# Encoder stage of a fused model: another order of TensorE's products, of the masked state on VectorE and of the query copy on ScalarE

## The reference, cut to what matters

```python
def _phi(t): return jax.nn.elu(t) + 1.0
def layer(h, p):
    q = _phi((h @ wq + bq_).reshape(b, s, H, DH))
    k = _phi((h @ wk + bk_).reshape(b, s, H, DH))
    v = (h @ wv + bv_).reshape(b, s, H, DH)
    kv = jnp.einsum('bshd,bshm->bhdm', k, v)
    z = 1.0 / (jnp.einsum('bshd,bhd->bsh', q, k.sum(axis=1)) + 1e-06)
    att = jnp.einsum('bshd,bhdm,bsh->bshm', q, kv, z).reshape(b, s, d)
    h = h + att @ wo + bo_
    h = _ln(h, g1_, be1_)
    y = jax.nn.gelu(h @ w1 + c1_, approximate=False) @ w2 + c2_
    return (_ln(h + y, g2_, be2_), None)
h, _ = jax.lax.scan(layer, x, params)
return _ln(h, gf, bef)
```

## Time and profile before

| what | value |
|---|---|
| median of 3 runs | 3285.73 us |
| profiled execution: span from its first to its last instruction | 3171.8 us |
| profiled execution's own time | not recorded; the median stands 113.9 us above the span |
| mean granted TensorE clock | 0.897 of full speed |
| first and last projection of the encoder (L3088) | 1516.7 and 2559.8 us |
| TensorE, VectorE, ScalarE, GpSimd busy over the span | 82%, 66%, 57%, 36% |

### The profile page before, as it was taken

One profiled execution on the slowest core, in us unless ns is written; L12 is line 12 of the kernel. 1 busy time (PEld: TensorE's weight loads), 2 busy tenths in 40 slices (PEclk: granted clock), 3 DMA queues, 4 the chain that ended last, 5 costly groups with the idle time before them and its releaser, 6 DMA issues.

```text
span 3171.8 us, 67664 instructions
## 1 busy us (share of the span) xinstructions
PE 2585.6 (82%) x25429; PEld 2010.4 (63%) x25429; DVE 2092.7 (66%) x7713; ACT 1796.5 (57%) x3508; POOL 1149.2 (36%) x1583
## 2 busy tenths in 40 slices
PE   7899988677797693587689999999999867875776
PEld 4466664455576472355578888888888755553555
DVE  6667758843578535533687777777777776336767
ACT  5344446333463342345479988899989744453443
POOL 4200004631754407755642222222222236555412
PEclk9799999789898895689799999999999987896997
DMA  9400000034100252144100000000000001441000
GB/s 276 125 3 3 3 2 1 31 94 135 34 17 25 76 142 65 49 126 138 32 16 13 1 13 13 1 13 13 1 13 1 1 2 42 126 137 28 22 2 28
DMA packets 134053, 147.94 MB, mean 47 GB/s; under 512 B 14817, under 2 KB 109922, under 8 KB 133730
## 3 DMA queue, kind: packets, MB, share of 16 engines
q1 hardware_dynamic: 106306, 71.13, 7.7%
q0 software_dynamic: 27424, 72.48, 7.6%
HBM read 77.63 MB, written 65.93 MB: 45 GB/s over the span
## 4 chain that ended last, share of the span: by engine, by line
PE 59%; DVE 19%; POOL 11%; issue 6%; ACT 4%; DMA 1%; SPq 0%; POOLq 0%; DVEq 0%; ACTq 0%
PE banks L3160 7%; PE banks L3147 5%; POOL results L1351 4%; POOL bins L1152 3%; PE banks L3092 3%; PE banks L3109 2%; PE banks L1900 2%; PE banks L3118 2%; PE banks L546 2%; PE banks L3128 1%; PE banks L3101 1%; PE banks L2926 1%; PE banks L3088 1%; DVE shared_floats L2050 1%; PE banks L2927 1%
## 5 line engine op out<-in xcount | busy, mean ns | idle before, releaser
L3238 POOL TENSOR_SCALAR shared_floats<-shared_floats 128x2 f32<-128x2 f32 x256 | 57.7, 225 | 710.0 <-DVE shared_floats L3229 709.3
L3160 PE MATMUL banks<-layer,shared_floats 128*128 128x128 f32 x2048 | 273.2, 277 | 0.0
L3474 ACT ACTIVATE shared_floats<-banks,layer 128x256 f32<-128x256 f32 x512 | 210.3, 471 | 90.9 <-PE banks L3147 90.9
L3160 PEld LDWEIGHTS banks<-layer,shared_floats 128*128 128x128 f32 x2048 | 251.7, 194 | 0.0
L3147 PE MATMUL banks<-shared_floats,layer 128*128 128x256 f32 x1024 | 243.9, 381 | 0.0
L3250 DVE TENSOR_SCALAR shared_floats<-banks,shared_floats 128x128 f32<-128x128 f32 x512 | 186.3, 405 | 58.7 <-POOL shared_floats L3240 58.7
L1351 POOL DMA_INDIRECT results<-results,result_rows x128 | 124.5, 973 | 256.8 <-DMA results<-shared_floats 219.5
L3226 DVE BATCH_NORM_STATS2 shared_floats<-banks 128x6 f32<-128x128 f32 x512 | 125.9, 287 | 122.3 <-PE banks L3160 118.8
L3147 PEld LDWEIGHTS banks<-shared_floats,layer 128*128 128x128 f32 x1024 | 185.9, 192 | 20.2
L3240 POOL TENSOR_TENSOR shared_floats<-shared_floats,neg_half 128x2 f32<-128x2 f32 x256 | 183.9, 718 | 21.3
L238 PE MATMUL banks<-ident,xn 128*128 128x128 f32 x320 | 65.4, 340 | 138.5 <-issue 74.8
(11 more groups left out here) (393 smaller groups left out, 7993.9 us busy)
## 6 DMA issues: line engine op xcount, KB each, us to landing
bins<-zero SPq DMA_DIRECT2D x1, 18176.0 KB, 86.6
shared_floats<-bins SPq DMA_DIRECT2D x32, 320.0 KB, 4.2
results<-shared_floats SPq DMA_DIRECT2D x32, 320.0 KB, 3.5
expert_weights<-in_dram_experts SPq DMA_DIRECT2D x32, 312.0 KB, 3.1
layer<-in_dram_layers SPq DMA_DIRECT2D x8, 902.0 KB, 4.7
bins<-zero SPq DMA_DIRECT2D x1, 5760.0 KB, 23.6
bins<-xn,f_bin_row POOLq DMA_INDIRECT x256, 2.2
results<-results,result_rows POOLq DMA_INDIRECT x128
```

The costliest lines, as they stand in the source:

```text
L3160: m = T.matmul(to, hidden[:, n * S + t * P:n * S + (t + 1) * P], w["w2"][:, tile(n)], start=False, stop=(n == NF - 1), skip_group_check=True)
L3474: m = A.activation(hidden[:, n * S:(n + 1) * S], k.bank[5 + half][:, part], ACT.Gelu, bias=w["c1"][:, n:n + 1])
```

## The change

On TensorE `project` is split in two: `project_q` now comes before `turn_xn2` and `project_kv` behind it; and the second narrow is split: its transpose and first two products come before `turn_att`, its last two behind it. On VectorE `mask_state(g)` moves from the start of round g+1 to round g, between the two `norm_apply` calls. On ScalarE the first half of `exps_q` becomes `lift_q` and moves ahead of `copy_h`. The work itself is the same.

```diff
--- before.py
+++ after.py
@@ -3075,7 +3075,7 @@
 
     T = k.nc.tensor
 
-    def project(u):
+    def project_q(u):
         w, h = layer_weights(k, u), turned(k, u)
         if u % B == 0:
             T.wait_ge(k.sem(f"e2_layer_in{u // B % 2}"), 16 * (u // B // 2 + 1))
@@ -3086,6 +3086,9 @@
         if u:
             T.wait_ge(k.sem("e2_exp_q"), u)
         T.matmul(k.bank[0][:, LOW], w["wq"], h, start=True, stop=True).then_inc(k.sem("e2_q_made"), 1)
+
+    def project_kv(u):
+        w, h = layer_weights(k, u), turned(k, u)
         if u:
             T.wait_ge(k.sem("e2_kv"), u)
         for t in range(QT):
@@ -3147,7 +3150,8 @@
                 m = T.matmul(k.bank[5 + half][:, part], w["w1"][:, tile(n)], h1[:, :], start=True, stop=True)
             m.then_inc(k.sem("e2_wide"), 1)
 
-    def narrow(u, t):
+    def narrow(u, t, begin=0, end=NF):
+
         w, hidden, h1_c2 = layer_weights(k, u), k.sb("e2_hidden", [P, NF * S]), k.sb(f"e2_h1_c2_{u % 2}", [P, S])
         to = k.bank[7][:, tile(t)]
         if t == 0:
@@ -3155,11 +3159,12 @@
             T.wait_ge(k.sem("e2_gelu"), 2 * u + 2)
             if u:
                 T.wait_ge(k.sem("e2_xn2"), u)
-        T.transpose(to, h1_c2[:, tile(t)], k.ident[:, :])
-        for n in range(NF):
+        if begin == 0:
+            T.transpose(to, h1_c2[:, tile(t)], k.ident[:, :])
+        for n in range(begin, end):
             m = T.matmul(to, hidden[:, n * S + t * P:n * S + (t + 1) * P], w["w2"][:, tile(n)],
                          start=False, stop=(n == NF - 1), skip_group_check=True)
-        if t == QT - 1:
+        if t == QT - 1 and end == NF:
             m.then_inc(k.sem("e2_narrow"), 1)
 
     def turn_xn2(u):
@@ -3188,18 +3193,22 @@
     for g in range(LEAVE + 2 * NC):
         if 1 <= g <= U2:
             sum_states(g - 1)
+        if g < U2:
+            if g > LEAVE:
+                T.wait_ge(k.sem("e2_left"), (g - LEAVE + 1) // 2)
+            project_q(g)
         if 4 <= g < U2 + 4:
             turn_xn2(g - 4)
         if g < U2:
-            if g > LEAVE:
-                T.wait_ge(k.sem("e2_left"), (g - LEAVE + 1) // 2)
-            project(g)
+            project_kv(g)
         if 1 <= g <= U2:
             attend(g - 1)
         if 3 <= g < U2 + 3:
             narrow(g - 3, 0)
         if 2 <= g < U2 + 2:
             turn_xn1(g - 2)
+        if 3 <= g < U2 + 3:
+            narrow(g - 3, 1, 0, NF // 2)
         if 1 <= g <= U2:
             turn_att(g - 1)
         if g < 2 * NC and g % 2 and g // 2 + 1 < NC:
@@ -3208,7 +3217,7 @@
         if g >= LEAVE and (g - LEAVE) % 2 == 0:
             leave((g - LEAVE) // 2)
         if 3 <= g < U2 + 3:
-            narrow(g - 3, 1)
+            narrow(g - 3, 1, NF // 2, NF)
         if 1 <= g <= U2:
             project_out(g - 1)
         if 2 <= g < U2 + 2:
@@ -3378,8 +3387,6 @@
             enter(g // 2 + 1)
         if s.after_routed and g < 2 * NC - 3 and g % 2:
             combine_first(k, s, g // 2 + 2)
-        if 1 <= g <= U2:
-            mask_state(g - 1)
         if g < U2:
             add_bias(g)
         if 1 <= g <= U2:
@@ -3403,6 +3410,8 @@
             norm_apply(k, "e2_xn2", g - 3, k.bank[7])
         if g < 2 * NC - 2 and g % 2 == 0:
             ln_apply(k, s, g // 2 + 1)
+        if g < U2:
+            mask_state(g)
         if 1 <= g <= U2:
             norm_apply(k, "e2_xn1", g - 1, k.bank[3][:, HIGH])
         if 3 * B <= g < 3 * B + 2 * NC and g % 2:
@@ -3428,14 +3437,17 @@
         A.wait_ge(k.sem("ln_turned"), n + 1)
         A.copy(k.sb("e2_hT", [P, N])[:, c * CH:(c + 1) * CH], k.bank[0][:, :]).then_inc(k.sem("ln_xnT"), 1)
 
-    def exps_q(u):
-        w, exp_q, q1 = layer_weights(k, u), k.sb("e2_exp_q", [P, S]), k.sb("e2_q_plus", [P, S])
+    def lift_q(u):
+        w, q1 = layer_weights(k, u), k.sb("e2_q_plus", [P, S])
         if u % B == 0:
             A.wait_ge(k.sem("e2_prepared"), u // B + 1)
         A.wait_ge(k.sem("e2_q_made"), u + 1)
         if u:
             A.wait_ge(k.sem("e2_qk"), u)
         a.count(A.activation(q1[:, :], k.bank[0][:, LOW], ACT.Identity, bias=w["bq1"]))
+
+    def exps_q(u):
+        w, exp_q = layer_weights(k, u), k.sb("e2_exp_q", [P, S])
         A.activation(exp_q[:, :], k.bank[0][:, LOW], ACT.Exp, bias=w["bq"]).then_inc(k.sem("e2_exp_q"), 1)
 
     def exps_k(u):
@@ -3482,6 +3494,8 @@
 
     enter(0)
     for g in range(LEAVE + 2 * NC):
+        if g < U2:
+            lift_q(g)
         if 4 <= g < U2 + 4:
             copy_h(g - 4)
         if g < U2:
```

## The result

The changed kernel takes **3240.72 us** (median of 4 runs, 3223.71 to 3246.47), the kernel before beside it 3284.05 us (4 runs, 3281.26 to 3286.63). That is 43 us faster by the medians. The ratio of the two on record is 0.9836 with an interval of 0.9811 to 0.9861, which makes it 46 to 62 us; the medians alone give 0.9868, just outside. So the change is faster beyond doubt, and its size is known to some 10 us. Forecast were 3242, 3222 to 3265, and faster at 0.91.

The account below looks back on a forecast made before the run. TensorE was taken to bound steady rounds, VectorE the first and last. Gains of 18 + 4.4 + 0.8 + 20.6 = 43.8, taken as 44, cut the span from 3171.8 to 3128; plus 113.9 gave 3242 us, range 3222 to 3265.

Parts of the forecast that it names:

- bias rounds: Eight rounds where VectorE adds L2_final's bias before the mask take 0.55 more; the move hides it, 4.4 us.
- the three old waits: TensorE's waits at turn_xn2 (0.13), turn_att (0.24) and attend (0.05), together 0.42 us a round, would all go.
- The new wait: TensorE before project_out, waiting for ScalarE's attT copy: 0.16 late plus 0.06 restart, taken as 0.25; bounds 0 and 0.43.
- What removes which wait: On TensorE, mask move removes attend's 0.05, query product ahead of turn_xn2 its 0.13, split narrow turn_att's 0.24.
- The edges: First and last rounds, bound by VectorE, gain 0.86 or 1.11 each, mean 0.98; 20.6 us, bounds 8 and 27.
- its three items: VectorE's edge loop: mask slot (0.32) and idle for attend (0.32) leave; xn1 is applied 0.33 or 0.08 later.
- C: Rival, chance 0.04: ScalarE's loop, laid out at 7.50, becomes the bound and the kernel slower, 3372 or 3290.
- Rival A: Wait before project_out as long as the three it replaces; only first and last rounds gain, 26 us: 3260; chance 0.18.
- D: Rival, chance 0.06: neutral, entering rounds give back the steady gain because the mask's wait holds VectorE; some 3286.
- B: Rival, chance 0.10: no wait arises before project_out, ScalarE's copy coming 0.2 earlier; steady rounds 7.3, time 3216.
- The table load: ScalarE, between q and attT copy: the row shows 1.28 us; the skill's 2.66 would make rounds some 8.9.
- What lies outside the span: The median's 113.9 us above the 3171.8 span, placed outside first and last instruction and carried over unchanged.

Follow-up runs that it names:

- second execution: The changed kernel run once more, unaltered, in the second series against the kernel before: 3117.26 us, ratio 0.9818.
- c1_one_ahead: The changed kernel with only the transpose and one product of the second narrow ahead of turn_att, three behind it: 3112.67 us, ratio 0.9800.
- e2_narrow_only: The kernel before with only the second narrow split around turn_att: 3155.33 us, ratio 0.9931.
- e1_mask_only: The kernel before with only mask_state moved: 3160.51 us, ratio 0.9948.
- c2_lift_behind_copy: The changed kernel with ScalarE's lift_q again behind copy_h: 3137.14 us, ratio 0.9881.
- the half widen: The changed kernel with half of widen, four passes of 256 columns, put ahead of project_out in every round: 3101.07 us, ratio 0.9776.

## Why the prediction was right

By its own steps, forecast against measured:

| term | forecast, us | measured, us |
|---|---|---|
| a steady round | 7.54 | 7.53 |
| 105 steady rounds | 18 | 19.8, the rest of the middle |
| bias rounds | 4.4 | 4.4 |
| prepare (one is added to a new layer's biases) | 0.8 | 0.9 (six rounds of 7.86) |
| entering rounds | 11.8 | 11.0 (14.2 in the second execution) |
| leaving rounds and the two before | 8.8 | 8.9 |
| sum | 43.8 | 45.1 |

The mechanism came as forecast: the three old waits gone, one new wait ahead of project_out that ScalarE's attT copy ends, and shorter bias, entering and leaving rounds. That 3242 meets the median of 3240.72 within 2 us is in part luck. The four times of the changed kernel spread over 23 us, the ratio on record makes the gain 54, and the same pair in the second series gained 55.

- *The new wait*: forecast 0.25, measured 0.22 (0.33 less 0.11). The forecast's 0.16 late and 0.06 to restart are these 0.22; the other 0.03 was for ScalarE's slots. The forecast had ScalarE ready at 4.63 and turn_att's result at 4.64. c1_one_ahead shows ScalarE ready 0.10 earlier: ScalarE was not late, turn_att and the copy behind it were the wait. The slots' "up to 0.06 later" did not come.
- *What removes which wait*: this step was wrong, without harm to the sum. I gave the 0.13 to the query product and the 0.05 to the mask. e2_narrow_only shows both gone by the split narrow, by its rows through the new wait itself. Waits that share a loop are not prices to be added: alone, q gives 0.05, the mask 0, the narrow 0.19, and the three together 0.19. The sum held because all three waits go: then the round is TensorE's own 7.29 and the new wait, whichever part removed which. My expectation for q alone was too high by the same mistake.
- *The bias*: right, and shown by e1_mask_only, where bias rounds cost 7.72 and not 8.27.
- *The edges*: right in sum, off in the parts. A leaving round fell from a mean of 10.12 (10.02 and 10.21) to 9.05, 1.07 against a forecast of 0.98; the measure holds seven of them (7.5) and the two before, which gave 1.4 where 1.0 was forecast. The mask alone gave 0.62 (9.5) where its three items come to 0.44, or to 0.56 without the new wait, which that run doesn't have. The narrow alone gave 0.21 (9.91) where I had 0.55; together they give 0.24 more than apart. Entering rounds fell, so the reading of VectorE's loop stands. The mask alone gave 5.7 there and the narrow alone 0.2 (147.0), so there too the parts gave more together than apart.
- *The rivals*: C's loop over ScalarE is real. Laid out at 7.50, it measures 7.42, 0.13 above TensorE's 7.29 and 0.11 below the changed kernel's round. c2_lift_behind_copy makes it the bound at 7.64. Rival A (7.7) and D (entering rounds that lose) are refuted by the rows; B (7.29) is what the half widen brings.
- *The table load*: the earlier trace rows had 1.28 us a load and the exponential 0.02 behind it. It is the same after, with 126 loads of each kind at a mean of 1283 ns. By the 2.66 a switch of the Trainium skill (ScalarE: Activation LUTs, What ACT_TABLE_LOAD costs) ScalarE's loop would be some 10.2 long by estimate (two times 1.38 more); it measures 7.42 in c1_one_ahead, and the measurement decides.
- *What lies outside the span*: this step was wrong. I put the 113.9 us between the span and the median outside the first and last instruction. Every run after shows 1.3 or 1.4 there (3237.99 less 3236.6). The profiled execution of before, at 3171.8, belongs with the times of the experiments (3173 to 3178), not with its own median. Its own time isn't on record, so this is inferred: its encoder starts at 1516.7, as in the experiments (1509.9 to 1533.1), while that of the changed kernel beside the result starts at 1630.1. Carrying the difference over unchanged did no harm, and that was luck: it lies in stages that the change doesn't touch.

## What to carry to other kernels

Lay the new order out from the pieces of one round, and put next to it the loop of each engine that hands work back; the longest loop is the round, and the next longest tells how far the gain can go (here 7.53, 7.42, 7.29). The three waits on one engine in one round were here mostly one lateness that showed in several places: a wait that is put in at one of them can pay for the others. And where a result must pass through another engine and come back, look for work that needs neither: the half widen was in the same round all along and was worth as much in the steady rounds (0.24) as the reordering (0.19), though not at the edges.

## What the runs showed of the hardware that was not expected

The same code took 3284 us beside the result and 3173 to 3178 in the three series of experiments, which ran on three different chips. The table of stretches ahead of the encoder (first the changed kernel beside the result, then the same kernel in the second series; columns as above):

```profile
0.00:1630.00 1630.00, 1217.52 (x14010) 865.57 (x14010) 916.75 (x3437) 652.07 (x1420) 582.88 (x676) 0.84 0.23 66
```

```profile
0.00:1522.00 1522.00, 1178.24 (x14010) 837.22 (x14010) 914.04 (x3437) 651.89 (x1420) 583.61 (x675) 0.87 0.24 70
```

It is the same 14010 passes in 108 us more, with VectorE's, ScalarE's and GpSimd's busy time alike within 3 us; TensorE stood still for 412 us instead of 344, and its mean granted clock was 0.84 instead of 0.87. Within the slow stretch the chain of waits has pieces that it can't assign, such as this one:

```profile
848.46 9.91 another core or an unknown queue
```

The encoder, at a mean clock of 0.99 and 0.98, shows no such thing (997.9 and 994.7). No run tells whether the chip (that of the result isn't on record) or the moment makes the difference, nor what these pieces wait for. It matters for reading: the gap between a span and a median can lie inside the span.

The second thing is the clock at the encoder's edges. Four of the fourteen profiles hold stretches of 3.4 us at 0.50 (1.2 GHz) in the last nine rounds, seven in all, and each makes its round 1.4 to 1.7 us longer; the other ten hold none there. This is why the last rounds of one kernel repeat less well than its middle; for the first fourteen it isn't the whole reason. What brings such a stretch about, no run shows.
